# First block of a decoder layer: squares and scaling on two engines, Wq loaded second, fold copies placed between the weights' split halves

## What is computed

```python
def rms_norm(x):
    eps = jnp.asarray(jnp.finfo(x.dtype).eps, x.dtype)
    return x * jax.lax.rsqrt(jnp.mean(x * x, axis=-1, keepdims=True) + eps)
...
xn = rms_norm(x)
q = jax.nn.silu(jnp.einsum('bnd,od->bno', xn, Wq))
k = jax.nn.silu(jnp.einsum('bnd,od->bno', xn, Wk))
v = jax.nn.silu(jnp.einsum('bnd,od->bno', xn, Wv))
g = jax.nn.sigmoid(jnp.einsum('bnd,od->bno', xn, Wg))
```

## Time and profile before

| | |
|---|---|
| time before, median of 3 runs | 843.66 us (843.52 to 843.76) |
| the profiled execution | 843.54 us |
| its span, first to last instruction | 841.7 us |
| PE busy | 821.1 us, 98% of the span |
| PEld, DVE, ACT, POOL busy | 658.0, 631.0, 290.7, 180.8 us |
| mean granted TensorE clock | 0.997 of 2.4 GHz |

### The profile page before, as it was taken

How to read it: one execution, slowest core, us unless ns; L and a number is a source line. 1 busy time by engine, 2 the same in 40 slices (tenths; PEclk the granted TensorE clock), 3 DMA queues, 4 the chain that set the end, 5 groups by cost and what they waited for, 6 DMA issues and landing times.

```text
span 841.7 us, 16104 instructions
## 1 busy us (share of the span) xinstructions
PE 821.1 (98%) x6386; PEld 658.0 (78%) x6386; DVE 631.0 (75%) x1392; ACT 290.7 (35%) x532; POOL 180.8 (21%) x156
## 2 busy tenths in 40 slices
PE   8999999999999999999999999999999999999996
PEld 6977677776887768776777788888888888888885
DVE  5587698899889998887957966666665666576576
ACT  5431263204432145303544423342323333232242
POOL 3046500663006630176312102100000000000121
PEclk9999999999999999999999999999999999999998
DMA  9300000100001000010220042102012021000001
GB/s 349 145 26 2 3 2 4 60 2 5 2 14 51 3 5 2 17 66 5 81 62 26 1 139 89 70 1 70 31 45 69 0 93 36 26 1 1 0 34 67
DMA packets 13092, 35.86 MB, mean 43 GB/s; under 512 B 1504, under 2 KB 2784, under 8 KB 12640
## 3 DMA queue, kind: packets, MB, share of 16 engines
q1 hardware_dynamic: 13024, 34.92, 12.1%
HBM read 30.26 MB, written 2.36 MB: 39 GB/s over the span
## 4 chain that ended last, share of the span: by engine, by line
PE 49%; DVE 2%; issue 1%; ACT 0%; POOL 0%; ACTq 0%; DVEq 0%
PE ps L259 15%; PE ps L260 15%; PE ps L261 15%; PE ps L1711 2%; PE ps L642 1%; PE ps L1702 0%; PE ps L1677 0%; PE ps L645 0%; PE ps L670 0%; DVE h_lo L374 0%; POOL roped L824 0%; ACT roped L979 0%; DVE su L543 0%; PE ps L1698 0%; PE ps L1542 0%
## 5 line engine op out<-in xcount | busy, mean ns | idle before, releaser
L824 POOL TENSOR_TENSOR roped<-prod 128x512 f32<-128x512 f32 x96 | 121.3, 1289 | 226.2 <-DVE prod L1175 226.1
L543 DVE TENSOR_TENSOR su<-sg,ps 128x512 f32<-128x512 f32 x96 | 66.0, 687 | 119.5 <-PE ps L261 117.3
L259 PE MATMUL ps<-y_hi,f_hi 128*128 128x512 f32 x384 | 150.8, 393 | 0.0
L261 PE MATMUL ps<-y_hi,f_lo 128*128 128x512 f32 x384 | 149.5, 389 | 0.0
L260 PE MATMUL ps<-y_lo,f_hi 128*128 128x512 f32 x384 | 149.4, 389 | 0.0
L403 ACT ACTIVATE sg<-ps 128x512 f32<-128x512 f32 x96 | 57.4, 598 | 249.1 <-PE ps L261 249.0
L1175 DVE TENSOR_TENSOR prod<-ps,ropeq 128x512 f32<-128x512 f32 x192 | 118.7, 682 | 21.7 <-PE ps L261 16.9
L259 PEld LDWEIGHTS ps<-y_hi,f_hi 128*128 128x128 f32 x384 | 72.1, 188 | 15.9 <-issue 1.1
L261 PEld LDWEIGHTS ps<-y_hi,f_lo 128*128 128x128 f32 x384 | 72.1, 188 | 15.0
L260 PEld LDWEIGHTS ps<-y_lo,f_hi 128*128 128x128 f32 x384 | 72.1, 188 | 14.9 <-issue 0.2
L259 PE MATMUL ps<-xT_hi,a_hi 128*128 128x512 f32 x192 | 79.2, 413 | 2.1 <-DVE prod L1175 2.1
(11 more groups left out here) (192 smaller groups left out, 1330.4 us busy)
## 6 DMA issues: line engine op xcount, KB each, us to landing
cb<-routing SPq DMA_DIRECT2D x32, 256.0 KB
f_raw<-in_L_ffn_gate_up_proj SPq DMA_DIRECT2D x8, 768.0 KB, 6.6
f_raw<-in_L_ffn_down_proj SPq DMA_DIRECT2D x8, 384.0 KB, 7.0
xb<-in_x SPq DMA_DIRECT2D x4, 512.0 KB, 4.1
lq<-in_L_xattn_Wq SPq DMA_DIRECT2D x1, 2048.0 KB, 14.3
x2T_all<-in_L_xattn_Wo SPq DMA_DIRECT2D x1, 2048.0 KB, 11.9
x2T_all<-x2T SPq DMA_DIRECT2D x4, 512.0 KB, 3.4
roped<-in_L_xattn_w_kc_q SPq DMA_DIRECT2D x1, 1536.0 KB, 10.0
```

What stands on the lines that cost most here:

```text
L259: pe.matmul(dst, l_hi, r_hi, start=first, stop=False, skip_group_check=check)
L261: return pe.matmul(dst, l_lo, r_hi, start=False, stop=last, skip_group_check=check)
L543: dve.tensor_tensor(su[:, k % 2], sg[:, k % 2], bank(2 * (k % 2) + 1), ALU.mult).then_inc(s_su, 1)
L824: pool.tensor_tensor(roped[:, 2 * (t % 4) + k], made(2 * t + k)[:, 0], made(2 * t + k)[:, 1], ALU.add)\
```

## The change

Everything in it belongs to the first block. Squares and sums of tiles 0 and 1 are made on VectorE with one `scalar_tensor_tensor` each, whose second output is the row sum; ScalarE keeps tiles 2 and 3. The root's last step signals a semaphore of its own, `s_root`, for which both engines wait; VectorE then scales tiles 0 and 1, ScalarE tiles 2 and 3 (a copy with a per-partition scale). TensorE waits for each half on its own semaphore. Wq is loaded right behind x. `keep_warm` runs eight products instead of nine. The copies `m_upper`/`m_lower` of folds 0 and 1 stand between the high and low parts of Wk, Wv and Wg.

```diff
-        own.step(dve.scalar_tensor_tensor(out=y, in0=u, scalar=1.5, in1=y, op0=ALU.add, op1=ALU.mult))
+        root = dve.scalar_tensor_tensor(out=y, in0=u, scalar=1.5, in1=y, op0=ALU.add, op1=ALU.mult)
+        if done is None:
+            own.step(root)
+        else:
+            root.then_inc(done, 1)
...
         load_x(0)
+        sp.dma_start(raw_w[0], a["L0_attn_Wq"]).then_inc(s_raw0[0], 16)
         sp.dma_start(ident[:], a["ident"]).then_inc(s_ident, 16)
...
             act.wait_ge(s_xb, 16 * b + 16)
-            for t in range(TILES):
+            for t in range(0 if b else 2, TILES):
                 act.activation(xn[:, t], xb[:, t], ACT.Square, accum_out=ss[:, t:t + 1]).then_inc(s_ss, 1)
...
             w_hi_out(0)
+            act.wait_ge(s_root, 1)
+            for t in (2, 3):
+                act.activation(xn[:, t], xb[:, t], ACT.Copy, scale=nt[:, 1, t:t + 1]).then_inc(s_xn23, 1)
             xT_hi_out(b, 0, s_xt, s_xthi)
             xT_hi_out(b, 1, s_xt, s_xthi)
-            for i in range(1, 4):
-                w_hi_out(i)
...
+            w_hi_out(1)
             m_upper(0)
+            w_hi_out(2)
+            m_upper(1)
             tanh(b, 0)
-            m_upper(1)
+            w_hi_out(3)
             tanh(b, 1)
...
         def rms(b):
-            dve.wait_ge(s_ss, 4 * b + 4)
+            if not b:
+                dve.wait_ge(s_xb, 16)
+                for t in range(2):
+                    own.step(dve.scalar_tensor_tensor(out=xn[:, t], in0=xb[:, t], scalar=1.0, in1=xb[:, t], op0=ALU.mult,
+                                                      op1=ALU.mult, accum_out=ss[:, t:t + 1]))
+            dve.wait_ge(s_ss, 4 * b + 2)
             own.need()
...
-            for t in range(TILES):
+            for t in range(TILES if b else 2):
                 dve.tensor_scalar(xn[:, t], xb[:, t], nt[:, 1, t:t + 1], None, ALU.mult).then_inc(s_xn, 1)
...
-            for i in range(1, 4):
-                w_lo_out(i)
...
+            w_lo_out(1)
             m_lower(0)
+            w_lo_out(2)
+            m_lower(1)
             silu(b, 0)
-            m_lower(1)
+            w_lo_out(3)
             silu(b, 1)
...
-                pe.wait_ge(s_in, 4 * b + t + 1)
+                if s_in is s_xn and b:
+                    pe.wait_ge(s_xn, 4 * b + t - 1)
+                elif s_in is s_xn:
+                    pe.wait_ge(s_xn if t < 2 else s_xn23, t % 2 + 1)
+                else:
+                    pe.wait_ge(s_in, 4 * b + t + 1)
...
-            keep_warm(9)
+            keep_warm(8)
```

More of the change, by code:

```diff
@@ L201, in build @@
     s_xn = sem("xn_ready")
+    s_xn23 = sem("first_xn_upper_ready")
+    s_root = sem("first_root_ready")
     s_xt = sem("xT_in_psum")
@@ L271, in rsqrt, with rsqrt4 @@
             own.step(dve.scalar_tensor_tensor(out=y, in0=t, scalar=1.5, in1=y, op0=ALU.add, op1=ALU.mult))
-    def rsqrt4(dve, own, value, y, u, w, half):
+    def rsqrt4(dve, own, value, y, u, w, half, done=None):
         own.need()
@@ L729, in _ @@
         sp.dma_start(x2f[:, 1536:2048], a["L0_xattn_W_kr"]).then_inc(s_raw2, 16)
-        for i, name in enumerate(("L0_attn_Wq", "L0_attn_Wk", "L0_attn_Wv", "L0_attn_Wg")):
+        for i, name in ((1, "L0_attn_Wk"), (2, "L0_attn_Wv"), (3, "L0_attn_Wg")):
             sp.dma_start(raw_w[i], a[name]).then_inc(s_raw0[i], 16)
@@ L1077, in rms @@
             own.step(dve.tensor_scalar(nt2[:, 0], ss, -0.5 / D, -0.5 * RMS_EPS, ALU.mult, ALU.add))
-            rsqrt4(dve, own, nt[:, 0], nt[:, 1], nt[:, 2], nt2[:, 1], nt2[:, 0])
-            own.need()
-            for t in range(TILES):
+            rsqrt4(dve, own, nt[:, 0], nt[:, 1], nt[:, 2], nt2[:, 1], nt2[:, 0], None if b else s_root)
+            if b:
+                own.need()
+            else:
+                dve.wait_ge(s_root, 1)
+            for t in range(TILES if b else 2):
                 dve.tensor_scalar(xn[:, t], xb[:, t], nt[:, 1, t:t + 1], None, ALU.mult).then_inc(s_xn, 1)
```

## The result

| | before | after |
|---|---|---|
| median, us (22 executions each) | 843.64 (843.36 to 844.23, and one of 2902.58) | 844.83 (844.26 to 845.51) |
| ratio, 95% interval | | 1.0014 (1.0008 to 1.002) |
| profiled execution, us | 843.54 | 844.55 |
| its span, us | 841.7 | 842.8 |

I had forecast 842.7, in a range of 842.1 to 843.6. The kernel got slower by 1.2 us, in the class that I had called most likely (within 0.2%) but with the other sign and outside the range. The interval leaves out "no change".

A forecast was written before the change was run, and what follows sets the result against it. It took TensorE (busy 98% of the span) as the bound, with the first projection's start at 11.62 setting the rest. Terms 0.75 + 0.25 = 1.00 us off 843.54 gave 842.5, as a median 842.7; range 842.1 to 843.6.

The forecast's parts named there:

- Squares, 0.75: First block: with two squares on VectorE beside ScalarE's two, the root starts 0.75 us earlier (bounds 0.25 and 0.80).
- rival of half rate: VectorE's accumulating squares run at half rate, so the gain is only 0.5 us, time 843.2; chance 15%.
- Scaling, 0.25: First block, behind the root: with scalings split over two engines, the last tile gains 0.25 us more (bounds 0.10 and 0.40).
- Wq second: First loads: Wq lands at about 5.1, hiding `w_hi` before the scalings; the loads moved back cost nothing, W_kr landing at 8.0.
- cover of 0.9: First folds: W_kr lands at 8.0 and the folds needing it start at 8.9, leaving 0.9 us.
- third rival: The gain is eaten on the way by a late W_kr, late x or a load-paced later stage; 843.4 to 843.7, chance 6%.
- Fold copies: Folds 0 and 1: moving their copies between the weights' high and low parts changes nothing either way.
- Warm-up: TensorE's start: one product fewer frees 0.45 us where it waits anyway, ending at 6.3, transposes at 7.6; gain nothing.
- slower rival: TensorE falls to its long pitch in the wait behind the shorter warm-up; slower by over 0.2%, 845.4; chance 5%.
- own sign of being wrong: Wrong if the first projection's start moves by under 0.4 or over 1.4 us, or by 1.0 without the span moving.
- moves the rest as a block: Behind the first projection's start at 11.62, all later work moves earlier equally unless something behind it is late.
- what is late next: Behind the first projection: TensorE's next needed load lands at 22.3 for a pass starting at 24.4, 2.1 us of cover.

The follow-up runs named there:

- e7: The changed kernel with Wq's load fifth again, as before the change; 845.00 us, ratio 1.0019.
- e2: The changed kernel with the lower copies of folds 2 and 3 back on ScalarE, restoring both engines' old instruction counts; 843.64 us, ratio 0.9998.
- e4: The changed kernel with the edits of e2 and e3 together; 842.97 us, ratio 0.9991.
- e9: The changed kernel with the copies of folds 0 and 1 in their old places; 845.08 us, ratio 1.0014.
- e3: The changed kernel with the two large loads of the query weights held back until the second fold is done; 843.82 us, ratio 1.0003.
- e6: The kernel of e4 with ident loaded second and Wq third; 842.70 us, ratio 0.9989.
- e1: The kernel before with two one-column memsets added at VectorE's idle start; 844.74 us, ratio 1.0013.
- e5: The kernel before with only the two large loads of the query weights held back until the second fold is done; 843.49 us, ratio 0.9996.
- e13: The kernel before with Wq's load second and nothing else changed; 843.96 us, ratio 1.0005.
- e10: The kernel before with one one-column memset added on VectorE; 843.70 us, ratio 1.0002.
- e12: The kernel before with thirty one-column memsets added on VectorE; 843.75 us, ratio 1.0005.
- e8: The kernel of e4 with Wq loaded from ScalarE's queue instead of SyncE's; 843.34 us, ratio 0.9997.

## Why the prediction was wrong, and where it was right

**Squares, 0.75.** Right and a little more. VectorE's passes took 0.42 each with a read of 0.08, and the root began at 5.21, 0.94 behind the square's start, where before it had been 1.74 behind (6.13 and 4.39): 0.80. Another 0.12 came from x landing earlier in this execution (4.27 for 4.39). The rival of half rate is out: its 0.68 a pass didn't come. The trace disagrees here with the rule of the Trainium skill ("Vector Engine (DVE) Microarchitecture Reference", section "Points that are easy to get wrong"): with fp32 operands in SBUF and an accumulator a pass took 0.42.

**Scaling, 0.25.** Right: two passes in 0.91 from 7.07, so tile 3 is ready at 7.98, 0.95 behind the root's end; 1.18 before (7.95 to 9.13). 0.23.

**Wq second.** The use was right (e7: without it the front gains nothing). "All costs nothing" was wrong. I took "loads land in order" with the bytes per microsecond of before; with Wq ahead W_kr lands at 8.8 in the kernel after, 9.2 in e2, 9.8 in e4, not at 8.0 (8.1 in e9 alone). My cover of 0.9 was spent in the profiled execution of the kernel after and overspent in e2, e3, e4 and e6, by 0.36 to 0.86 us. This is my third rival, the gain "eaten on the way", and I had given it 6%; its 843.4 to 843.7 was still too low for what came. Why W_kr is late by more than Wq's bytes stays open: ident's place is not it (e6).

**Fold copies.** Nothing, right (e9).

**Warm-up.** Nothing in the profiled execution, but not with the 1.3 us to spare that I gave it. I read the clock as "1.00 from the start". The passes of the warm-up say otherwise: each starts 0.43 us behind the one before it up to 4.0 us and 0.21 from there in the kernel before, and up to 6.4 us in the kernel after. The trace's own record of the granted clock begins only there, at 4.03 and 6.41, with 1.00; the views print 1.00 for the time before it too, where there is no record. So the warm-up ended at 7.47, not at 6.3, 0.10 ahead of the transposes. By an estimate from the 0.21 a ninth product (two passes) would have ended at 7.9 and held them up by 0.3. The place of the turn differs between executions of otherwise equal starts: with nine products the warm-up ended at 6.73 in the kernel before, the earliest of six profiles, and at 7.97 in e1; with eight at 6.39 to 7.95, and in e2, the last of these, the first transpose came 0.65 behind VectorE's scaling where it is 0.50 in the others. My slower rival (the long pitch behind the warm-up) did not happen: the projections behind 10.46 are 0.23 apart.

**The step that failed.** The prediction's own sign of being wrong came true: the first projection moved by 1.16 and the span did not follow. The step is "whatever makes that start earlier moves the rest as a block, as long as nothing behind it is late", with "what is late next" answered from data loads alone. Three things were late that aren't data in a tile:

- TensorE's next 16 KB of instructions. The kernel before had next to no cover there (17.2 to 17.4 against 17.37), so 1.1 us of lead shrank to 0.2. Shown by e3 and e5, and by e13 from the other side.
- The 8 KB fetch on queue 14, which VectorE's two more instructions moved from behind the last output into it: 0.7 us. Shown by e1 and e2 for the count, by e10 and e12 for the place.
- 0.4 us at 376. It comes and goes with the same two instructions (there in the kernel after, e1, e3, e7 and e9, not in e2, e4, e5, e6, e8, e10, e12, e13). That a fetch is behind this too is only argued: queue 14 has one at 376.99 before and at 377.02 after, both behind the product's start, and in e12, which lacks the loss, at 366.38.

The net count I could have had before: two passes of squares, each with its read, for two scalings less makes 1392 + 2. I looked only at durations, and my slower rival was a clock.

**The numbers.** The front was worth 1.16, more than the 1.00 of the sum. With the three losses taken out (e6) 0.8 us are left, 0.09%; there the folds wait 0.53 for W_kr, and the first projection leads by 0.69 (10.93 for 11.62). That my figure of 842.7 is also the median of e6 proves nothing for its working.

## What to carry to other kernels

When a stall at the front is removed, ask what the engine needs next besides data: its own instruction blocks come by DMA too, and bulk loads issued ahead can hold them back (14.72 for 11.79 us here). Where a gain is below a microsecond, count instructions on each engine too, since two more can put a fetch into the last transfer; the kernel before, with as many tiny instructions added where the engine is idle, shows that cost by itself. And a load moved forward is a new order for all behind it: price the last one of the group from a run, not from the old rate.

## What the runs showed of the hardware

- An 8 KB instruction fetch inside the last 512 KB output made it land 0.7 us later (3.3 for 2.6 us from issue, in all five profiles with a fetch there), though its packet takes 0.31 us; at the end 1 KB packets came one at a time, 0.042 us apart.
- A 16 KB fetch for TensorE started 2.9 to 3.3 us later behind queued bulk loads (14.72 for 11.79 in e3; 14.83 for 11.52 in e5), and the engine went on 2.3 to 2.6 us after the start. The Trainium skill ("Runtime: NRT & Kernel Launch", section "Instruction fetch mechanics") calls the cost of such a boundary "mostly hidden"; here fold 3 lost 0.9 us to one.
- With the 256 KB load of Wq (rows of 2 KB) second in the queue, the window of 4 to 8 us moved 317 and 320 GB/s at a DMA share of 1.01 in the kernel after and e13 (378 in e9), against 404 at the same share with it fifth.
- `scalar_tensor_tensor` of 128x256 fp32 with an accumulator takes 0.42 us on VectorE, as long as a plain product (420 ns), plus a read of 0.08 that the next pass overlaps (starts 0.35 us apart).
- TensorE's passes of 256 columns went from 0.43 to 0.21 us apart in every run, with the warm-up begun at 1.2 us in each: at 4.0 us in the kernel before, at 6.4 in the kernel after, at 7.4 in e2.
